# The order of SyncE's transfers in a graph transformer layer

## The chip, the cores and the metric

The kernel runs on one core of a Trainium2 chip. The metric is the time of one execution on the device in microseconds, and the median of the runs is quoted.

## What is computed

Four message-passing layers over one graph of 6,250 nodes with 256 features and 106,250 edges, sorted by destination: two graph convolutions, a graph attention layer with four heads, and a graph transformer layer. The change touches the last, and one transfer in the first:

```
q = x1 @ Wq + bq;  k = x1 @ Wk + bk;  v = x1 @ Wv + bv
logits2 = einsum('ec,ec->e', q[d2], k[s2]) / sqrt(256)
alpha2 = segment_softmax(logits2, d2)
out = segment_sum(v[s2] * alpha2[:, None], d2)
out = prelu(out + x1 @ Wskip + bskip)
```

## The kernel before

The edges are cut into 52 groups of 2,048, each as 16 steps (u = 0 to 15) of 128 edges. As edges are sorted by destination, the destinations of a group lie in a window of 128 nodes. `relrow`, in HBM, holds for each edge its place in that window as int16; it is written once in the first layer (lines 292 to 294) from the tile `rr` of seven columns of 128, of which the last is filled to 64 partitions only.

The last layer (`transformer_layer`, line 1772) works on three groups at a time, each at another stage. In pass k it scores group k, works out the softmax maxima of group k-1 (the "chain"), and sums group k-2 (the "agg"). `passes` (line 1809) writes out the first three passes and the last ones, and runs a loop over bodies of eight passes between. Every engine has a `body` for one pass; `parts` (line 1822) says which stages it has; `lead` is the preparation of group k+1.

- GpSimd gathers the source rows of each step from HBM into one of four buffers `G` (line 1841), as soon as the group four back is summed.
- TensorE does for each step a score matmul (L2198: the window `win` picked out by the one-hot `ohT` into `psA`) and an aggregation matmul (L2208), and between them the small transposes of the chain. It waits for the window of its group once, ahead of step 0 (line 2233). Score(u) waits until dot(u-2) is done.
- VectorE does for each step a dot product (L1943: `G` with `psA`), and the one-hot of the next group (L1918). It builds `ohT` (L1923) in four parts at steps 7, 10, 13 and 15 from `relb`, the row of places copied to all 128 partitions. At step 4 it scans with the mask `mkr` (L2031). At steps 1 to 12 it works out the node results of group k-2; the last of them is L1983, after which `s_res` is raised. A pass ends with two scans (L2142, L2146).
- ScalarE takes the exponentials and weighs the one-hots.
- SyncE issues the transfers. It handles them in program order and waits at semaphores in between. Per group there are the places (`relb`, 512 KB, four buffers, L1868), the window (`win`, 128.5 KB, two buffers, L1865), the mask (`mkr`, 1.5 KB, two buffers, L1885), the loads of `skip` and `xa` for the next node block (128 KB each, L1848 and L1849) and the store of the result (128 KB, L1855). Before the window of group k+1, SyncE waits until all scores of group k-1 are done (`s_pa`), before the places for a maximum of an earlier group (`s_s1`), before the mask for `s_s2`. The loads and the store wait for `s_res` (`turn`, line 1857).

So SyncE's body k, before, is: places of k+1, window of k+1, mask of k, extra windows if a group needs them, then `turn` for the group k-2: wait for `s_res`, loads, store.

Of the kernel before, what the change touches and what calls it, by code (L numbers as in the profile page):

```python
# [22 lines left out]
P = 128  # L23
# [8 lines left out]
NC = NG * U  # L32
# [8 lines left out]
UW = 16  # L41
GW = UW * P
NGW = NC // UW
# [58 lines left out]
def hold(m, eng):  # L102

    eng.sem_inc(m.held[str(eng.engine)], 1)  # L104
# [6 lines left out]
def load_wide(nc, m, eng, g, keys):  # L111

    lim = {"d0": (0, 0, N - 1), "nwin": (1, 1, NT), "base": (2, 0, NGW + NT), "last": (3, 0, N - 1), "xb": (4, 0, NT)}
    return [nc.s_assert_within(eng.value_load(m.ctw[0:1, bass.ds(g * TW + k, 1)]) & TABLE_BITS, lo, hi,
                               skip_runtime_bounds_check_because=TABLE_FITS)
            for k, lo, hi in (lim[n] for n in keys)]


def first_layer(nc, m, a):
# [13 lines left out]
    with ExitStack() as c:  # L133
# [36 lines left out]
        rr = sb("rr", [P, NCH, P], I16)  # L170
# [29 lines left out]
        @block.gpsimd  # L200
        def _(pool):
            nc.gpsimd.memset(m.ones[:], 1.0)
            nc.gpsimd.memset(m.eps[:], LN_EPS)
            nc.gpsimd.memset(m.ident[:], 0.0).then_inc(s_set, 1)
            pool.wait_ge(s_set, 1)
            nc.gpsimd.affine_select(out=m.ident[:], in_=m.ident[:], compare_op=ALU.not_equal, fill=1.0,
                                    base=0, pattern=[[-1, P]], channel_multiplier=1)
            nc.gpsimd.iota(m.iota[:], [[1, P]], base=0, channel_multiplier=0, allow_small_or_imprecise_dtypes=True)
            nc.gpsimd.iota(m.iotap[:], [[1, 1]], base=0, channel_multiplier=1, allow_small_or_imprecise_dtypes=True)
            nc.gpsimd.memset(stage[:], 0.0)  # L210
            nc.gpsimd.memset(al[:], 0.0)
            nc.gpsimd.memset(h[:, :, D:AW], 0.0)
            nc.gpsimd.memset(zrow[:], 0.0).then_inc(s_set, 1)
            nc.gpsimd.memset(acc, 0.0).then_inc(s_accz, 1)
            pool.wait_ge(s_si, 16)
            pool.wait_ge(s_z1, 16)
            pool.wait_ge(s_ast, 16)
            for j in range(NLB):
                pool.wait_ge(s_t1[j], 16)
            for g in range(NGW):  # L220
                b = g % NBW
                width = D if g < NBW else AW
                if g >= NBW:
                    pool.wait_ge(s_done, g - NBW + 1)
                if g == NBW:
                    pool.wait_ge(s_col, 16)
                for u in range(UW):
                    pool.indirect_dma_start(G[:, b, u, 0:width], None, m.t1,  # L228
                                            IOA(ap=m.srcI[:, g * UW + u:g * UW + u + 1], axis=0)).then_inc(s_g[b][u // QW], 16)
            pool.wait_ge(s_done, NGW - NBW + 1)  # L230
            pool.wait_ge(s_fin, 16)
            for u in range(EARLY2):
                pool.indirect_dma_start(m.gathered(D)[:, 0, u, :], None, m.t2, IOA(ap=m.srcI[:, u:u + 1], axis=0)).then_inc(m.ahead2[u // QW], 16)

        @block.sync
        def _(sp):
# [53 lines left out]
            sp.dma_start(part[:], m.wsum.rearrange("(g n) -> g n", n=SLOTS)).then_inc(s_part, 16)  # L290
            sp.wait_ge(s_rr, 1)
            places = m.relrow.rearrange("(c w e) -> w c e", w=P, e=P)
            sp.dma_start(places[:, 0:NC // P, :], rr[:, 0:NC // P, :]).then_inc(s_z, 16)
            sp.dma_start(places[0:NC % P, NC // P, :], rr[0:NC % P, NC // P, :]).then_inc(s_z, 16)
            sp.wait_ge(s_dis, 1)
            with nc.allow_non_contiguous_dma(reason="three columns of the table"):
                sp.dma_start(rows(m.t1)[:, :, D:AW], facs[:]).then_inc(s_col, 16)
# [27 lines left out]
            with sp.Fori(0, NGW) as k:  # L325
                d0, last = load_wide(nc, m, sp, k, ("d0", "last"))
                nwin, past = load_pack(nc, m, sp, k)
                base = past + k
# [4 lines left out]
            base, last = load_wide(nc, m, sp, NGW, ("base", "last"))  # L333
# [5 lines left out]
            sp.wait_ge(s_st, base * ST + (ST + 16))  # L339
            sp.wait_ge(s_fin, 16)  # L340
            hold(m, sp)
            sp.wait_ge(s_z, 16 * 9)

        @block.vector
        def _(dve):
# [1426 lines left out]
def transformer_layer(nc, m):  # L1772
# [4 lines left out]
    with ExitStack() as c:  # L1777
# [7 lines left out]
        mkr = sb("mkr", [1, 2, 3 * (P + 1)])  # L1785
# [11 lines left out]
        s_mk = [sem(f"mk{b}") for b in range(2)]  # L1797
# [24 lines left out]
        def parts(k):  # L1822
            if not isinstance(k, int):
                return True, True, True, True
            return k < NGW, 1 <= k <= NGW, k >= 2, k + 1 < NGW
# [3 lines left out]
        @block.gpsimd  # L1829
        def _(pool):  # L1830
            nc.gpsimd.memset(run[:], -BIG)
            nc.gpsimd.memset(Lb[:], -BIG)
            nc.gpsimd.memset(stage[:], 0.0).then_inc(s_zero, 1)
            for g in range(NGW):
                b = g % NBW
                if g >= NBW:
                    pool.wait_ge(s_ok, g - NBW + 1)
                for u in range(EARLY4 if g == 0 else 0, UW):
                    if g >= NBW and u % QW == 0:
                        pool.wait_ge(s_aq, (g - NBW) * NQ + u // QW + 1)  # L1840
                    pool.indirect_dma_start(G[:, b, u, :], None, m.t4, IOA(ap=m.srcI[:, g * UW + u:g * UW + u + 1],  # L1841
                                                                           axis=0)).then_inc(s_g[b][u // QW], 16)

        @block.sync
        def _(sp):

            def load(n, start):
                sp.dma_start(skip[:], m.sk[bass.ds(start, P), :]).then_inc(s_own, 16)  # L1848
                sp.dma_start(xa[:], m.xa[bass.ds(start, P), :]).then_inc(s_own, 16)  # L1849

            def store(n, start):
                sp.wait_ge(s_res, n + 1)
                sp.wait_ge(s_st, n * ST + ST)
                hold(m, sp)
                sp.dma_start(m.out[bass.ds(start, P), :], o[:]).then_inc(s_st, 16)  # L1855

            def turn(n, start, before):
                sp.wait_ge(s_res, n + 1)
                hold(m, sp)
                load(n + 1, start)  # L1860
                store(n, before)

            def window(k, r):
                d0, = load_wide(nc, m, sp, k, ("d0",))
                sp.dma_start(win[:, r, :], m.qk[bass.ds(d0, P), :]).then_inc(s_win[r], 16)  # L1865

            def places(k, b):
                sp.dma_start(relb[:, b % 4, :], m.relrow[bass.ds(k * (UW * P), UW * P)].partition_broadcast(P)).then_inc(s_rb[b % 4], 16)  # L1868

            def body(k, kq, kh, b, past):  # L1870
                logits, chain, agg, lead = parts(k)
                if lead:
                    if not (isinstance(k, int) and k < 3):
                        sp.wait_ge(s_s1, k - 2)
                        hold(m, sp)
                    places(k + 1, b + 1)
                    if agg or chain:
                        sp.wait_ge(s_pa, k * UW)
                        hold(m, sp)
                    window(k + 1, (b + 1) % 2)  # L1880
                if logits:
                    if agg:
                        sp.wait_ge(s_s2, k - 1)
                        hold(m, sp)
                    sp.dma_start(mkr[:, b % 2, :], m.rmask[bass.ds(k * (3 * (P + 1)), 3 * (P + 1))]  # L1885
                                 .rearrange("(a n) -> a n", a=1)).then_inc(s_mk[b % 2], 16)
                    d0, = load_wide(nc, m, sp, k, ("d0",))
                    nwin, xb = load_pack(nc, m, sp, k)
                    with sp.If(nwin > 1):
                        with sp.Fori(1, nwin) as i:  # L1890
                            sp.wait_ge(s_xpa, (xb + i - 1) * UW + 1)
                            hold(m, sp)
                            sp.dma_start(winx[:], m.qk[bass.ds(window_start(nc, d0, i), P), :]).then_inc(s_xwin, 16)
                if agg:
                    d0, last = load_wide(nc, m, sp, k - 2, ("d0", "last"))
                    nwin, xb = load_pack(nc, m, sp, k - 2)
                    base = xb + (k - 2)
                    turn(base, d0, last)
                    with sp.If(nwin > 1):
                        with sp.Fori(1, nwin) as i:  # L1900
                            turn(base + i, window_start(nc, d0, i), window_start(nc, d0, i - 1))

            sp.sem_inc(s_xpa, 1)
            sp.sem_inc(s_st, ST)
            places(0, 0)
            window(0, 0)
            load(0, 0)
            passes(sp, body)
            base, last = load_wide(nc, m, sp, NGW, ("base", "last"))
            store(base, last)  # L1910
            sp.wait_ge(s_st, (base + 2) * ST)
            hold(m, sp)
# [521 lines left out]
```

## Time and profile before

| | |
|---|---|
| median of 3 runs | 6158.78 us (6152.38 to 6185.52) |
| the profiled execution, its span | 6170.1 us, 6168.3 us |
| busy: TensorE, VectorE, GpSimd, ScalarE | 3904.2, 2719.5, 3232.2, 718.2 us |
| mean granted TensorE clock | 0.762 |
| SyncE's queue | 170437 packets, 185.56 MB |
| GpSimd's queue | 159744 packets, 441.43 MB |

The page of the profile shows these for one execution. The span is the time from its first to its last instruction. Beside the page, the trace was asked for busy time by stretch, for who waited for whom, and for timelines of single engines. In a timeline a row has the start, the length, engine, line and operation, what it writes and reads, and in brackets how long the engine was idle before it and what ended this. A wait for several semaphores is put down to the one that came last by the profile, which can be another than the real one. DVE is VectorE, PE is TensorE, POOL is GpSimd, SPq is SyncE's queue.

### The profile page before, as it was taken

To read this page: it belongs to the slowest core of one execution; us is meant where nothing else is said; L and a number is where in the kernel's file an instruction comes from. 1 tells how busy PE (TensorE), PEld (TensorE's weight loads), DVE (VectorE), ACT (ScalarE), POOL (GpSimd) and SP (SyncE) were. 2 spreads that over 40 slices of the span, in tenths; PEclk is the share of its full clock that TensorE was granted. 3 is DMA by queue.
4 is the path that set the end of the run, shared out by engine and by line. 5 is a ranking of instruction groups with operands and counts; after the bars stand their busy time and mean duration, and the time that the engine had idled before them with its cause. 6 is when DMAs were issued, how large, how long until landed. Compare 5 with 4: busy or idle time off the path is not lost. (4 is left out here: it accounts for less than half of the span.)

```text
span 6168.3 us, 73822 instructions
## 1 busy us (share of the span) xinstructions
PE 3904.2 (63%) x14562; PEld 2847.0 (46%) x14563; DVE 2719.5 (44%) x9904; ACT 718.2 (12%) x2361; POOL 3232.2 (52%) x3351
## 2 busy tenths in 40 slices
PE   3555555563556655554667666767674777777777
PEld 2343434342444444443455555555552555555555
DVE  5443434342333233332444444444453555555555
ACT  3000000000000000000111111101110212222122
POOL 5466666644555555554444444444433555555553
PEclk8677777776777777776777776777786888888889
DMA  7344444433333333332333333333322444343432
GB/s 182 80 107 106 107 105 107 106 86 88 106 107 106 106 107 107 107 101 87 89 94 97 93 97 93 96 95 95 96 78 84 113 119 122 111 119 112 118 115 84
DMA packets 334355, 636.43 MB, mean 103 GB/s; under 512 B 86166, under 2 KB 213124, under 8 KB 333828
## 3 DMA queue, kind: packets, MB, share of 16 engines
q0 software_dynamic: 159744, 441.43, 27.5%
q1 hardware_dynamic: 170437, 185.56, 9.6%
q8 instruction: 177, 2.90, 0.2%
q10 hardware_dynamic: 3648, 3.67, 0.2%
q14 instruction: 349, 2.86, 0.2%
HBM read 565.59 MB, written 64.79 MB: 102 GB/s over the span
## 5 line engine op out<-in xcount | busy, mean ns | idle before, releaser
L1211 POOL DMA_INDIRECT G<-t,srcI x828 | 807.6, 975 | 914.2 <-DVE g_Gp L1425 676.3
L1841 POOL DMA_INDIRECT G<-t,srcI x824 | 785.7, 953 | 629.6 <-PE g_ps L2208 371.7
L228 POOL DMA_INDIRECT G<-t,srcI x832 | 820.7, 986 | 516.1 <-issue 238.7
L859 POOL DMA_INDIRECT G<-t,srcI x828 | 793.6, 958 | 536.7 <-ACTq L1133 298.8
L2198 PE MATMUL g_psA<-g_win,g_ohT 128*128 128x257 f32 x1664 | 614.1, 456 | 374.7 <-DVE g_L L1943 177.6
L737 PE MATMUL g_ps<-G,g_oh 128*128 128x257 f32 x1664 | 555.6, 500 | 142.8 <-DVE g_oh L587 142.8
L1554 PE MATMUL g_psA<-g_win,g_ohT 128*128 128x4 f32 x1664 | 345.1, 328 | 439.1 <-issue 416.4
L1943 DVE CUSTOM_DVE_ANT_0 g_junk<-G,g_psA 128x257 f32<-128x257 f32 x832 | 348.5, 419 | 557.9 <-DMA G<-t,srcI 239.2
L1554 PEld LDWEIGHTS g_psA<-g_win,g_ohT 128*128 128x128 f32 x1664 | 359.6, 316 | 459.6 <-issue 459.1
L2208 PE MATMUL g_ps<-G,g_oh 128*128 128x257 f32 x1664 | 558.2, 422 | 0.0
L2198 PEld LDWEIGHTS g_psA<-g_win,g_ohT 128*128 128x128 f32 x1664 | 321.7, 217 | 511.2 <-DVE g_L L1943 222.6
L737 PEld LDWEIGHTS g_ps<-G,g_oh 128*128 128x128 f32 x1664 | 415.7, 258 | 290.2 <-DVE g_oh L587 186.4
L1088 PE MATMUL g_ps<-G,g_oh 128*128 128x256 f32 x1664 | 510.6, 455 | 0.0
L1601 PE MATMUL g_ps<-g_Gp,g_oh 128*128 128x264 f32 x1664 | 412.4, 396 | 21.3 <-issue 21.1
L1088 PEld LDWEIGHTS g_ps<-G,g_oh 128*128 128x128 f32 x1664 | 376.9, 235 | 96.2 <-issue 33.9
L2208 PEld LDWEIGHTS g_ps<-G,g_oh 128*128 128x128 f32 x1664 | 352.3, 215 | 84.8 <-issue 24.9
L1314 DVE TENSOR_TENSOR g_oh<-iota,g_relx 128x512 f32<-128x512 f32 x208 | 136.0, 689 | 560.1 <-DMA G<-t,srcI 500.7
L1601 PEld LDWEIGHTS g_ps<-g_Gp,g_oh 128*128 128x128 f32 x1664 | 313.6, 193 | 97.3 <-issue 44.0
L966 DVE TENSOR_SCALAR g_oh<-iota,g_relx,g_wx 128x128 f32<-128x128 f32 x832 | 228.7, 349 | 185.9 <-DMA G<-t,srcI 89.7
L594 DVE SCALAR_TENSOR_TENSOR g_a<-g_own,g_stage 128x256 f32<-128x256 f32 x53 | 25.7, 485 | 567.4 <-ACT g_stage L809 566.0
L587 DVE TENSOR_SCALAR g_oh<-iota,g_relx,g_wx 128x128 f32<-128x128 f32 x832 | 240.3, 362 | 32.5 <-issue 22.8
L2300 ACT ACTIVATE g_oh<-g_oh,g_p 128x128 f32<-128x128 f32 x832 | 248.7, 387 | 6.4
(372 smaller groups left out, 4825.9 us busy)
## 6 DMA issues: line engine op xcount, KB each, us to landing
G<-t,srcI POOLq DMA_INDIRECT x3328
g_relb<-relrow SPq DMA_DIRECT2D x104, 512.0 KB
t<-g_t SPq DMA_DIRECT2D x53, 132.0 KB, 1.7
g_rec<-t SPq DMA_DIRECT2D x53, 132.0 KB
g_own<-t SPq DMA_DIRECT2D x53, 129.5 KB
x<-g_o SPq DMA_DIRECT2D x53, 128.5 KB
g_rec<-x SPq DMA_DIRECT2D x53, 128.5 KB
t<-g_t4r SPq DMA_DIRECT2D x53, 128.5 KB, 2.0
```

The costliest lines, as they stand in the source:

```text
L228: pool.indirect_dma_start(G[:, b, u, 0:width], None, m.t1, IOA(ap=m.srcI[:, g * UW + u:g * UW + u + 1], axis=0)).then_inc(s_g[b][u // QW], 16)
L737: last = nc.tensor.matmul(ps[:, 0:CW], oh[:, u, :], G[:, b, u, 0:CW], start=(u == 0), stop=(u == UW - 1))
L859: pool.indirect_dma_start(G[:, b, u, :], None, table, IOA(ap=m.srcI[:, g * UW + u:g * UW + u + 1], axis=0)).then_inc(s_g[b][u // QW], 16)
L1088: last = nc.tensor.matmul(ps[:, 0:D], oh[:, u, :], G[:, b, u, :], start=(u == 0), stop=(u == UW - 1))
L1211: pool.indirect_dma_start(G[:, b, u, :], None, m.t3, IOA(ap=m.srcI[:, g * UW + u:g * UW + u + 1], axis=0)).then_inc(s_g[b], 16)
L1554: last = nc.tensor.matmul(psA[:, u * H:u * H + H], ohT[:, u, :], win[:, b % 2, :], start=True, stop=True)
L1601: last = nc.tensor.matmul(ps[:, 0:AGW], oh[:, b1, u, :], Gp[:, b1, u, :], start=(u == 0), stop=(u == UW - 1))
L1841: pool.indirect_dma_start(G[:, b, u, :], None, m.t4, IOA(ap=m.srcI[:, g * UW + u:g * UW + u + 1], axis=0)).then_inc(s_g[b][u // QW], 16)
L1943: nc.vector.tensor_tensor_reduce(out=junk[:, u % 2, :], in0=G[:, b, u, :], in1=psA[:, u % 2, 0:RW], scale=1.0, scalar=0.0, op0=ALU.mult, o ...
L2198: nc.tensor.matmul(psA[:, u % 2, 0:RW], ohT[:, u, :], win[:, r, :], start=True, stop=True).then_inc(s_pa, 1)
L2208: last = nc.tensor.matmul(ps[:, r, 0:RW], oh[:, b2, u, :], G[:, b2, u, :], start=(u == 0), stop=(u == UW - 1))
L2300: last = nc.scalar.activation(src[:, u, :], src[:, u, :], ACT.Copy, scale=p[:, r, u:u + 1])
```

## The change

In the last layer SyncE's body k waits for the result of group k-2 (`s_res`) first, and then issues the window of group k+1, the loads and the store of `turn`, the places of group k+2 (instead of k+1) and the mask of group k. Ahead of the loop two rows of places are issued, for groups 0 and 1. For the wait of the places, `s_s1` is asked for k-1 instead of k-2. In passes 0 and 1, which have no result to wait for, the rest is issued in the same order. Extra windows of the group stay ahead of all this; no group of this input needs one.

In the first layer GpSimd sets the last column of `rr` to zero, so that `relrow` is stored whole with one transfer instead of two.

```diff
             nc.gpsimd.memset(al[:], 0.0)
+            nc.gpsimd.memset(rr[:, NC // P, :], 0)
...
-            sp.dma_start(places[:, 0:NC // P, :], rr[:, 0:NC // P, :]).then_inc(s_z, 16)
-            sp.dma_start(places[0:NC % P, NC // P, :], rr[0:NC % P, NC // P, :]).then_inc(s_z, 16)
+            sp.dma_start(places, rr[:]).then_inc(s_z, 16)
...
-            sp.wait_ge(s_z, 16 * 9)
+            sp.wait_ge(s_z, 16 * 8)
...
             def body(k, kq, kh, b, past):
                 logits, chain, agg, lead = parts(k)
-                if lead:
-                    if not (isinstance(k, int) and k < 3):
-                        sp.wait_ge(s_s1, k - 2)
-                        hold(m, sp)
-                    places(k + 1, b + 1)
-                    if agg or chain:
-                        sp.wait_ge(s_pa, k * UW)
-                        hold(m, sp)
-                    window(k + 1, (b + 1) % 2)
                 if logits:
-                    if agg:
-                        sp.wait_ge(s_s2, k - 1)
-                        hold(m, sp)
-                    sp.dma_start(mkr[:, b % 2, :], m.rmask[bass.ds(k * (3 * (P + 1)), 3 * (P + 1))]
-                                 .rearrange("(a n) -> a n", a=1)).then_inc(s_mk[b % 2], 16)
                     d0, = load_wide(nc, m, sp, k, ("d0",))
...
                     base = xb + (k - 2)
-                    turn(base, d0, last)
+                    sp.wait_ge(s_res, base + 1)
+                    hold(m, sp)
+                if lead:
+                    if agg or chain:
+                        sp.wait_ge(s_pa, k * UW)
+                        hold(m, sp)
+                    window(k + 1, (b + 1) % 2)
+                if agg:
+                    load(base + 1, d0)
+                    store(base, last)
+                if lead:
+                    if not isinstance(k, int) or k + 2 < NGW:
+                        if not (isinstance(k, int) and k < 2):
+                            sp.wait_ge(s_s1, k - 1)
+                            hold(m, sp)
+                        places(k + 2, b + 2)
+                if logits:
+                    if agg:
+                        sp.wait_ge(s_s2, k - 1)
+                        hold(m, sp)
+                    sp.dma_start(mkr[:, b % 2, :], m.rmask[bass.ds(k * (3 * (P + 1)), 3 * (P + 1))]
+                                 .rearrange("(a n) -> a n", a=1)).then_inc(s_mk[b % 2], 16)
...
             places(0, 0)
+            places(1, 1)
             window(0, 0)
```

## Rows read from the trace of the kernel before

**Rows 1.** Busy time in a stretch of the last layer: window, length, engines, clock, DMA.
```profile
5050.00:5400.00 350.00, 262.98 (x997) 189.31 (x998) 202.91 (x948) 74.15 (x245) 194.78 (x205) 0.88 0.41 115
```

**Rows 2.** Tile view of the window: score matmuls, durations, first and last start.
```profile
L2198 PE MATMUL g_psA<-g_win,g_ohT x1664: 378/380/797, 4690.1 to 6137.4; 128*128 128x257 f32 x185
```

**Rows 3.** Waits from 4800 to 6100 us: total, times, longest.
```profile
POOL G L1841 <- PE g_ps L2208: 345.1, 114, 6.1
...
DVE g_junk L1943 <- PE g_psA L2198: 155.7, 151, 3.8
```

**Rows 4.** Timeline of VectorE, one pass: start, length, line, idle before.
```profile
5314.87 0.42 DVE L1983 TENSOR_TENSOR g_o<-g_o,g_v 128x256 f32<-128x256 f32 x1
...
5320.31 0.42 DVE L1943 CUSTOM_DVE_ANT_0 g_junk<-G,g_psA 128x257 f32<-128x257 f32 x1 [1.08 <-issue]
```

**Rows 5.** Timeline of SyncE's queue, the same pass.
```profile
5315.61 0.37 SPq L1848 DMA_DIRECT2D g_skip<-sk  x1
...
5318.49 0.36 SPq L1855 DMA_DIRECT2D out<-g_o  x1
5320.12 0.01 SPq L1868 DMA_DIRECT2D g_relb<-relrow  x1
5323.14 0.71 SPq L1865 DMA_DIRECT2D g_win<-qk  x1
5326.03 0.01 SPq L1885 DMA_DIRECT2D g_mkr<-rmask  x1
```

**Rows 6.** Timeline of TensorE, the same pass.
```profile
5318.06 0.69 PE L2198 MATMUL g_psA<-g_win,g_ohT 128*128 128x257 f32 x2
```

**Rows 7.** Timelines of VectorE and TensorE, the shortest and the longest distance.
```profile
4905.91 0.41 DVE L1983 TENSOR_TENSOR g_o<-g_o,g_v 128x256 f32<-128x256 f32 x1
...
4908.86 0.70 PE L2198 MATMUL g_psA<-g_win,g_ohT 128*128 128x257 f32 x2 [0.29 <-issue]
...
5010.73 0.42 DVE L1983 TENSOR_TENSOR g_o<-g_o,g_v 128x256 f32<-128x256 f32 x1
...
5018.64 1.22 PE L2198 MATMUL g_psA<-g_win,g_ohT 128*128 128x257 f32 x2 [4.42 <-issue]
```

**Rows 8.** Timeline of SyncE's queue, one pass later.
```profile
5346.96 0.34 SPq L1868 DMA_DIRECT2D g_relb<-relrow  x1
5348.12 0.64 SPq L1865 DMA_DIRECT2D g_win<-qk  x1
```

**Rows 9.** The page, part 6: issues of transfers, KB each, median us to landing.
```profile
t<-g_t SPq DMA_DIRECT2D x53, 132.0 KB, 1.7
...
t<-g_t4r SPq DMA_DIRECT2D x53, 128.5 KB, 2.0
```

**Rows 10.** Timelines of VectorE and SyncE, a tight pass.
```profile
5097.51 0.46 DVE L1983 TENSOR_TENSOR g_o<-g_o,g_v 128x256 f32<-128x256 f32 x1
...
5107.07 0.28 SPq L1885 DMA_DIRECT2D g_mkr<-rmask  x1
...
5108.28 0.47 DVE L2031 TENSOR_TENSOR_SCAN g_run<-g_mkr,g_run,g_psR 1x128 f32<-1x128 f32 x1
```

**Rows 11.** Timelines of SyncE's queue and VectorE, start of the layer.
```profile
4685.24 0.35 SPq L1868 DMA_DIRECT2D g_relb<-relrow  x1
4686.17 0.35 SPq L1865 DMA_DIRECT2D g_win<-qk  x1
...
4689.57 1.71 DVE L1923 TENSOR_SCALAR g_ohT<-g_relb,iotap 128x512 f32<-128x512 int16 x4 [3.42 <-DMA g_relb<-relrow]
```

**Rows 12.** Timeline of GpSimd, start of the kernel.
```profile
0.73 0.20 POOL L202 MEMSET ones<- 128x128 f32 x1 [0.29 <-POOLq L2428]
```

**Rows 13.** Timeline of VectorE: three dots with a wait, idle before in brackets.
```profile
4808.79 0.42 DVE L1943 CUSTOM_DVE_ANT_0 g_junk<-G,g_psA 128x257 f32<-128x257 f32 x1 [2.46 <-PE g_psA L2198]
...
5310.00 0.42 DVE L1943 CUSTOM_DVE_ANT_0 g_junk<-G,g_psA 128x257 f32<-128x257 f32 x1 [3.66 <-DMA G<-t,srcI]
...
5992.90 0.42 DVE L1943 CUSTOM_DVE_ANT_0 g_junk<-G,g_psA 128x257 f32<-128x257 f32 x1 [2.70 <-PE g_psA L2198]
```

More of the change, by code:

```diff
@@ L1897, in body @@
                     base = xb + (k - 2)
-                    turn(base, d0, last)
+                    sp.wait_ge(s_res, base + 1)
[20 more added lines that the diff above has]
+                                 .rearrange("(a n) -> a n", a=1)).then_inc(s_mk[b % 2], 16)
+                if agg:
                     with sp.If(nwin > 1):
```

## The prediction

> **What bounds the kernel now.** I started with the granted clock and busy time by stretch. In a steady 350 us of the last layer, TensorE is busy 75% at a granted clock of 0.88, VectorE 58% and GpSimd 56% [rows 1]. So none of them is full. The score matmuls of that layer run from 4690.1 to 6137.2 us [rows 2], which over 52 groups is 27.8 us per group, and only this layer changes much. Next come the waits. VectorE's dots wait for TensorE 151 times and GpSimd for TensorE's aggregation 114 times [rows 3]. TensorE and VectorE form a ring: a dot needs its score, and score(u) may run only two dots ahead. No row has anyone of size waiting for a SyncE transfer. The transfers are off the path now, and the question is whether the change puts one on it.
>
> So I put SyncE's queue beside the ring. One group's batch begins when VectorE's last node step (L1983) ends: at 5314.87 + 0.42 = 5315.29 [rows 4]. SyncE issues skip at 5315.61, the store at 5318.49, the relative row (places) at 5320.12, the window at 5323.14 and the mask at 5326.03 [rows 5]. **The kernel before already issues all of these in one burst behind the result**, because the next body's lead-in follows the previous turn at once. What the program calls two groups ahead is therefore, in time, the burst in which the row leaves today: before, body k+1 sends the row of k+2, after, body k does, both behind the result of pass k. The same goes for load and store. Two things really move: the window and the mask each leave one whole group later (window k+1 behind the result of pass k, not k-1), and inside the burst the window goes from last but one to first.
>
> **Window, the main term.** When is it needed? Score(0) of the next pass starts at 5318.06 in this pass, 2.77 us after the result [rows 6]. Over the 47 passes that begin between 4.8 and 6.1 ms this distance runs from 2.54 us (4905.91 + 0.41 to 4908.86) to 7.49 us (5010.73 + 0.42 to 5018.64) [rows 7]; I put them in order and the middle one is 3.4. VectorE can absorb some lateness, since it scans and reads its table there: score(0) ends at 5318.06 + 0.69 = 18.75 but dot(0) starts at 5320.31 [rows 4, 6]. For dot(1), the smaller margin of the two, I found 1.0 to 1.6 us in the tight passes. I take 1.2.
>
> When does it land? SyncE needs about four small steps from result to skip issue, 0.32 us (5315.29 to 5315.61) [rows 4, 5]. The window needs those and a table read. From the row's issue to the window's is 1.16 us where SyncE is quick (5346.96 to 5348.12) and 3.02 us where it is slow (5320.12 to 5323.14) [rows 5, 8]. Without the row's own issue (0.34, 0.7) that is 0.8 to 2.3 us, so with the 0.32 the window leaves 1.1 to 2.7 us after the result. Nearest transfers of 128 KB: 1.7 and 2.0 us from issue to landing [rows 9]. Landing is then 2.8 to 4.7 us after the result; I also allow 6, for gathers that share the engines. I then ran every one of the 47 passes through max(0, landing - start of score(0) - its margin). The sums: landing at 3.5 us costs 0; at 4.0, 1 us in all; at 4.5, 5 us; at 5.0, 14; at 5.5, 25; at 6.0, 39. **I take 4.5, so +5 us**, nearest to the slow SyncE rows since 5315 and most passes look like them; ends 0 and +39.
>
> Here the Trainium skill speaks against the change: DMA: Bandwidth & Descriptors, Rules for kernel authors, says to issue a DMA early, compute, and wait late. The trace agrees that the present order has no window wait. The same page (Anatomy of one DMA, a fit for GpSimd's path) gives 2.0 us plus bytes over 436e3; for 131,584 B that is an estimate of 2.3 us against the 1.7 and 2.0 of the rows. By it landings would be 0.3 to 0.6 later and the term about +10 instead of +5.
>
> **Mask.** It too loses a group of lead, and it is now behind the 512 KB row instead of the window. Its reader is the forward scan at step 4 (L2031). In a tight pass the result ends at 5097.51 + 0.46 = 5097.97, the mask is issued at 5107.07 and the scan runs at 5108.28 [rows 10]; today that scan reads the mask of the burst before, afterwards it would read this one, 1.2 us after its issue. The issue keeps its place in the burst, but the row ahead of it leaves some 1.5 us later than now: 5320.12 - 5315.29 = 4.8 [rows 4, 5] becomes 6.3, and with the 4.3 us that the first row of the layer took (below) it is in at 10.6 us after the result, against a scan at 10.3 here. No row shows the mask's own landing. Bounds: 0, where step 4 is later (the scan comes after 11 us in most passes), and 1.0 us in each of the 12 tightest, +12. Behind a mask wait stand VectorE's next dots. I take +3, near the low end, as a pass made late by the window has its scan late too.
>
> **Row, load, store.** The row slips behind window, loads and store by about 1.5 us; its reader, the first ohT build of a pass, comes at step 7, three steps after that scan, and the one row wait that I found is at the layer's start (3.42 us [rows 11]). Load and store move by the same 1.5 us; readers are steps 6 and 11. Cost 0; if that cover were gone, one transfer per group, 2 us or about 100 in all.
>
> **Layer start.** Rows 0 and 1 now go ahead of window 0. Row issue at 4685.24, window at 4686.17 [rows 11], first score at 4690.1 [rows 2]. One more issue (0.93 us) and one more 512 KB: the row took 4.3 us to the first ohT build (4689.57 [rows 11]), less the 2.0 of a small one, 2.3 us. The first score is held by ohT anyway. Between 0 and +3.3; I take +1.
>
> **First layer.** One transfer issue fewer on SyncE, whose issues take 0.3 to 0.7 us each [rows 5, 8], and one memset of 128 x 128 more on GpSimd (0.20 us for one of float32 [rows 12]). Both are one-off steps in the opening of a 6 ms kernel: between -0.7 and +0.2, taken as 0.
>
> **Sum.** 5 + 3 + 1 + 0 = +9 us. Against the profiled execution, 6170.1 us with a span of 6168.3, that is 6179; this execution is 11.3 us (0.2%) above the median of 6158.8, and the terms do not scale with that, so the forecast for the median is 6158.8 + 9 = **6168 us**, +0.15%. A measurement of this kernel can tell about 0.5% (31 us) from no change, so the likely verdict is "same".
>
> **Rivals.** (1) *Nothing measurable moves at all.* The window lands by 3.5 us and the mask before the scan: 6160. For it: the quick SyncE rows, and that the burst is already one. (2) *The window wait becomes the new turn of the ring, slower.* It decides from a landing of about 5.7 us after the result, where the sum passes 31. For it: in slow stretches SyncE takes 3.02 us for steps that it does elsewhere in 1.16, the window now leaves behind such steps, and gathers share its engines. Against: in 28 of the 47 passes score(0) starts later than 3.0 us after the result. Price 39 at 6 us plus 4 for mask and start: 6202; the skill's early-issue rule above would point here. (3) *A gain.* VectorE waits about 2.5 us for TensorE at step 3 or 4 in 13 passes (2.46 the first, 2.70 the last [rows 13]), just when the tail of the burst, window and mask, is in flight. If that is the transfers' doing and goes with the window's move: 13 x 2.4 = 31 less, +9, gives 6137. Against: longer waits stand at steps 8 and 9, where SyncE issues nothing (3.66 us at 5310.00 [rows 13]; that row names a gather, but step 9 waits for no gather), and the big transfer stays.
>
> **How the numbers follow.** Forecast as worked out 0.50 and rival 1 0.20, both inside 0.5%; rival 2 0.18; rival 3 0.07; 0.05 for what I have not seen, slower by 0.02 and faster by 0.03. So faster 0.10, same 0.70, slower 0.20. The range goes from rival 3 to rival 2: 6138 to 6204.
>
> **What would show it.** Right: the window first in SyncE's burst, 1.1 to 2.7 us after L1983 ends; new, short TensorE idle times ahead of score(0) put down to the window's transfer, in under half of the passes, and L2031 with a wait under 1 us in some; distance from result to dot(0) in tight passes (5.0 now) at most 6; the spacing of row and load unchanged. Wrong: dot(0) at 6.5 or more in most passes (rival 2); no window wait at all (rival 1); or step 3 and 4 waits gone (rival 3). The prediction fails as a whole if the long waits at steps 8 and 9 hang on SyncE's transfers after all, for then every shift in the burst counts, in either direction.

## The result, and the profile after

The changed kernel took 6184.51 us in the median (6161.43 to 6210.51), the kernel before, run beside it, 6168.45. The ratio is 1.003, with an interval of 1.0022 to 1.0039: **18.5 us slower**, 0.3%, inside the 0.5% that I had called "same". (Differences in us are here and below the ratio applied to the time of before.) I had forecast +9. The size of the effect is twice the forecast, and this section and the next find where the other half sits.

One execution scatters by more than the effect. The profiled one of the changed kernel took 6174.2 us with a span of 6172.4, only 4 us above that of before, so sums over one trace say how the work moved, and the medians say what it cost.

The window's tile view of the changed kernel answers [rows 2] (form, durations in ns, first and last start). L2207 is the score matmul; the changed file is nine lines longer there. The lines under it say what its engine had waited for, in us and times:
```profile
L2207 PE MATMUL g_psA<-g_win,g_ohT x1664: 377/380/797, 4688.0 to 6141.3; 128*128 128x257 f32 x185
...
  DMA g_win<-qk: 55.1, 19
```
The layer's score matmuls run over 1453.3 us instead of 1447.3. And there is a wait that the kernel before had nowhere inside the layer: TensorE waits for the window's transfer.

Waits of the changed kernel from 4800 to 6100 us, the same view as [rows 3] (total, times, longest):
```profile
POOL G L1841 <- PE g_ps L2217: 368.5, 127, 6.2
...
DVE g_junk L1952 <- PE g_psA L2207: 140.9, 159, 4.5
...
PE g_psA L2207 <- DMA g_win<-qk: 31.0, 17, 3.1
...
DVE g_run L2040 <- DMA g_mkr<-rmask: 0.3, 1, 0.3
```
The profile puts 17 passes, 31.0 us in all, down to the window. That count is a low one: of many window transfers this trace holds only some of the 16 events that tell of completion, and the wait is then called "issue". Without names, TensorE stands idle for over 1 us ahead of score(0) in 35 of 46 passes, where before it did so in 6 of 48 (five of these six are the turns of the loop, every eighth pass, and they stay). The mask is waited for once, for 0.3 us. The row of places, the loads and the store stand in no wait of the steady part.

A steady stretch, as in [rows 1], barely differs; clock 0.87 instead of 0.88:
```profile
5050.00:5400.00 350.00, 262.09 (x986) 191.81 (x985) 201.52 (x934) 73.90 (x244) 193.67 (x203) 0.87 0.41 114
```

Now one pass. SyncE's queue after the result of a tight pass, which answers [rows 5]. The result (L1992, L1983 before) ends at 5096.11 + 0.42 = 5096.53:
```profile
5098.88 0.69 SPq L1865 DMA_DIRECT2D g_win<-qk  x1
5099.67 0.44 SPq L1848 DMA_DIRECT2D g_skip<-sk  x1
5100.20 0.38 SPq L1849 DMA_DIRECT2D g_xa<-xa  x1
5102.00 0.01 SPq L1855 DMA_DIRECT2D out<-g_o  x1
5102.77 0.71 SPq L1868 DMA_DIRECT2D g_relb<-relrow  x1
```
The order is the new one, window first, and the window leaves 2.35 us after the result. TensorE and VectorE of the same pass, as in [rows 4, 6]:
```profile
5096.78 0.60 PE L2207 MATMUL g_psA<-g_win,g_ohT 128*128 128x257 f32 x2
...
5101.36 0.70 PE L2207 MATMUL g_psA<-g_win,g_ohT 128*128 128x257 f32 x2 [1.96 <-issue]
...
5102.45 1.06 PE L2207 MATMUL g_psA<-g_win,g_ohT 128*128 128x257 f32 x2
```
```profile
5100.28 0.19 DVE L2155 TENSOR_TENSOR_SCAN g_W<-mk,g_F 128x16 f32<-128x16 f32 x1 [0.24 <-DVE g_F L2151]
5102.09 0.42 DVE L1952 CUSTOM_DVE_ANT_0 g_junk<-G,g_psA 128x257 f32<-128x257 f32 x1 [1.62 <-PE g_psA L2207]
...
5103.56 0.42 DVE L1952 CUSTOM_DVE_ANT_0 g_junk<-G,g_psA 128x257 f32<-128x257 f32 x1 [0.83 <-PE g_psA L2207]
```
Score(0) starts 4.83 us after the result, where a tight pass of before had 2.54 to 2.77 [rows 6, 7], and VectorE, done with its scans at 5100.47, waits 1.62 us for it. The profile puts TensorE's 1.96 us down to "issue" here, so this pass is none of the 17; the trace holds 4 of the 16 completion events of its window. As score(0) starts 2.48 us after the window's issue, and in the 17 passes the same distance is 2.38 in the middle (1.1 to 4.1), I read it as a wait for the window all the same.

A second price shows in the same rows: score(1) takes 1.06 us where the matmuls ahead of the wait took 0.60, and dot(1) waits another 0.83. Over 49 passes, score(1) takes over 1.0 us in 20; before it did so in 7. Busy time and clock by stretch (PE is the first busy time, the clock the third number from the end):
```profile
5098.50:5101.30 2.80, 0.90 (x4) 0.30 (x2) 1.20 (x6) 0.39 (x1) 1.21 (x3) 1.00 0.59 165
5101.30:5105.00 3.70, 3.64 (x10) 2.95 (x11) 1.32 (x7) 0.00 (x0) 2.72 (x3) 0.62 0.83 234
```
After a stretch in which TensorE was busy for 0.90 of 2.80 us, the granted clock falls from 1.00 to 0.62 in the mean of the next 3.7 us, so mostly its 1.2 GHz level, and the first steps of the pass go at that pace.

Over all passes that have a result ahead of them (49 or 50), the middle distances from the result, before and after: window issue 7.48 and 2.77 us (before, that one was meant for the pass after next, a whole group earlier); score(0) 3.5 and 5.38; dot(0) 6.34 and 6.91; places issue 4.94 and 6.22; mask issue 9.25 and 7.12; mask scan 11.78 and 11.95. The median period of a pass goes from 27.26 to 27.55.

The layer's start answers [rows 11]: two rows of places, then the window, and the wait for the places is as long as before.
```profile
4681.43 0.83 SPq L1868 DMA_DIRECT2D g_relb<-relrow  x2
4682.84 0.34 SPq L1865 DMA_DIRECT2D g_win<-qk  x1
...
4685.73 1.67 DVE L1932 TENSOR_SCALAR g_ohT<-g_relb,iotap 128x512 f32<-128x512 int16 x4 [3.38 <-DMA g_relb<-relrow]
```
From the first row to the first score is 4688.0 - 4681.43 = 6.6 us; before it was 4690.1 - 4685.24 = 4.9 [rows 2, 11]. So the second row costs up to 1.7 us, once, which no median here can resolve.

### The profile page after: what moved, and what is told of

Read it like the earlier page. It is cut to its first block and busy times, and to the rows that moved or that the text cites. A ratio compares the mean times of both kernels' runs of the same rounds, so it can differ in the third digit from the quotient of the medians.

```text
span 6172.4 us, 73818 instructions
## 1 busy us (share of the span) xinstructions
PE 3919.8 (64%) x14562; PEld 2866.9 (46%) x14563; DVE 2718.8 (44%) x9904; ACT 718.8 (12%) x2361; POOL 3231.6 (52%) x3352
## 3 DMA queue, kind: packets, MB, share of 16 engines
q0 software_dynamic: 159744, 441.43, 27.4%
q10 hardware_dynamic: 3648, 3.67, 0.2%
## 5 line engine op out<-in xcount | busy, mean ns | idle before, releaser
L2207 PE MATMUL g_psA<-g_win,g_ohT 128*128 128x257 f32 x1664 | 626.0, 464 | 390.6 <-DVE g_L L1952 167.7
L737 PE MATMUL g_ps<-G,g_oh 128*128 128x257 f32 x1664 | 556.4, 500 | 141.9 <-DVE g_oh L587 141.9
L2207 PEld LDWEIGHTS g_psA<-g_win,g_ohT 128*128 128x128 f32 x1664 | 333.5, 222 | 513.3 <-issue 231.1
L2217 PE MATMUL g_ps<-G,g_oh 128*128 128x257 f32 x1664 | 569.8, 430 | 0.0
```

The source lines that it names most:

```text
L737: last = nc.tensor.matmul(ps[:, 0:CW], oh[:, u, :], G[:, b, u, 0:CW], start=(u == 0), stop=(u == UW - 1))
L2207: nc.tensor.matmul(psA[:, u % 2, 0:RW], ohT[:, u, :], win[:, r, :], start=True, stop=True).then_inc(s_pa, 1)
L2217: last = nc.tensor.matmul(ps[:, r, 0:RW], oh[:, b2, u, :], G[:, b2, u, :], start=(u == 0), stop=(u == UW - 1))
```

## The experiments

**Parts of the change.** Four kernels ran beside the kernel before, at 6143.52 us there. `e1_window_late` makes one part alone: the kernel before, but with the window behind the result.

```diff
-                    if agg or chain:
-                        sp.wait_ge(s_pa, k * UW)
-                        hold(m, sp)
-                    window(k + 1, (b + 1) % 2)
+                    if not agg:
+                        if chain:
+                            sp.wait_ge(s_pa, k * UW)
+                            hold(m, sp)
+                        window(k + 1, (b + 1) % 2)
...
-                    turn(base, d0, last)
+                    sp.wait_ge(s_res, base + 1)
+                    hold(m, sp)
+                    if lead:
+                        sp.wait_ge(s_pa, k * UW)
+                        hold(m, sp)
+                        window(k + 1, (b + 1) % 2)
+                    load(base + 1, d0)
+                    store(base, last)
```


> The kernel before with one thing changed: the window of group k+1 is issued behind the result, first in the burst, as in the changed kernel; places, mask and the first layer stay as they were. Theory (the window wait is the cost): ratio to before 1.002 to 1.004 (+12 to +25 us), TensorE waits for the window in 15 or more passes. Rival (the cost is the mask behind the row, or the order of the burst as a whole): 1.000 to 1.001.

Measured: 6166.73 us, ratio 1.0039 (1.0026 to 1.0051), +24 us. Waits of the layer's steady part (4800 to 6100 us), in an execution of 6137.98 us, the fastest of the six: the row shows where TensorE waits, and only the medians show the price.
```profile
PE g_psA L2206 <- DMA g_win<-qk: 40.6, 22, 3.6
```
The window alone costs what the whole change costs.

`e2_window_early` is the converse: the changed kernel with everything in its new place but the window, which leaves ahead of the wait for the result again.

```diff
+                if lead:
+                    if agg or chain:
+                        sp.wait_ge(s_pa, k * UW)
+                        hold(m, sp)
+                    window(k + 1, (b + 1) % 2)
                 if logits:
                     d0, = load_wide(nc, m, sp, k, ("d0",))
...
                     sp.wait_ge(s_res, base + 1)
                     hold(m, sp)
-                if lead:
-                    if agg or chain:
-                        sp.wait_ge(s_pa, k * UW)
-                        hold(m, sp)
-                    window(k + 1, (b + 1) % 2)
```


> The changed kernel with the window issued again ahead of the result, one group earlier; everything else as changed. Theory (the window wait is the cost): ratio to before 0.9995 to 1.001, no wait for the window. Rival (mask behind the row, places, first layer): stays at 1.002 to 1.004.

Measured: 6143.08 us, ratio 0.9996 (0.9987 to 1.0005), and no wait for the window in the steady part. Undoing this part undoes the loss, to within an interval of -8 to +3 us.

`e3_row_whole` makes the edit of the first layer alone, in the kernel before (the memset and the two hunks of the diff about `rr` and `s_z`).

> The kernel before with the first layer's part of the change alone: last column of rr set to zero, relrow stored with one transfer. Every theory: ratio 1.000, within 0.001. A ratio above 1.002 would mean that the cost lies there and not in the last layer.

Measured: 6147.66 us, ratio 1.0005 (0.9994 to 1.0016): nothing.

`e4_mask_early` is the changed kernel with the mask issued early again, ahead of the wait for the result.

```diff
                 if logits:
+                    if agg:
+                        sp.wait_ge(s_s2, k - 1)
+                        hold(m, sp)
+                    sp.dma_start(mkr[:, b % 2, :], m.rmask[bass.ds(k * (3 * (P + 1)), 3 * (P + 1))]
+                                 .rearrange("(a n) -> a n", a=1)).then_inc(s_mk[b % 2], 16)
+                if logits:
                     d0, = load_wide(nc, m, sp, k, ("d0",))
...
-                if logits:
-                    if agg:
-                        sp.wait_ge(s_s2, k - 1)
-                        hold(m, sp)
-                    sp.dma_start(mkr[:, b % 2, :], m.rmask[bass.ds(k * (3 * (P + 1)), 3 * (P + 1))]
-                                 .rearrange("(a n) -> a n", a=1)).then_inc(s_mk[b % 2], 16)
```


> The changed kernel with the mask issued again one group earlier, ahead of the wait for the result; window late. Theory (the window wait is the cost, the mask term that I put at +3 us is near 0): ratio 1.002 to 1.004, as the change itself. Rival (the mask behind the 512 KB row costs a third or more): 1.001 to 1.002.

Measured: 6167.81 us, ratio 1.0041 (1.0028 to 1.0054). With the mask out of the way nothing is won back. The interval is 16 us wide, too wide to tell my +3 from 0; the one mask wait of 0.3 us in the changed kernel's trace is what says that it was nearly 0.

**The size of the lag.** `e5_window_last` takes the window from the front of the burst to its end, behind the 512 KB row; nothing else changes:

```diff
-                if lead:
-                    if agg or chain:
-                        sp.wait_ge(s_pa, k * UW)
-                        hold(m, sp)
-                    window(k + 1, (b + 1) % 2)
                 if agg:
                     load(base + 1, d0)
...
                                  .rearrange("(a n) -> a n", a=1)).then_inc(s_mk[b % 2], 16)
+                if lead:
+                    if agg or chain:
+                        sp.wait_ge(s_pa, k * UW)
+                        hold(m, sp)
+                    window(k + 1, (b + 1) % 2)
```

`e6_table_ahead` takes the other direction: SyncE reads the window's address from its table before it waits for the result, so that the window leaves sooner.

```diff
                     base = xb + (k - 2)
+                    if lead:
+                        dw, = load_wide(nc, m, sp, k + 1, ("d0",))
                     sp.wait_ge(s_res, base + 1)
                     hold(m, sp)
...
-                    window(k + 1, (b + 1) % 2)
+                    if agg:
+                        sp.dma_start(win[:, (b + 1) % 2, :], m.qk[bass.ds(dw, P), :]).then_inc(s_win[(b + 1) % 2], 16)
+                    else:
+                        window(k + 1, (b + 1) % 2)
```


> The changed kernel with the window issued last in the burst, behind row and mask. In the changed kernel the mask's issue is at 7.1 us after the result in the median; a window issued there lands at about 10. By the step model of the prediction (landing less start of score(0) less 1.2 us, summed over 47 passes; score(0) started at 3.9 us in the mean) that is 5 us a pass: +200 to +260 us, ratio 1.032 to 1.042. Rival (the ring absorbs most of it, since its long waits at steps 8 and 9 move into the wait): under +120 us, ratio under 1.02.

> The changed kernel with the read of the window's table entry moved ahead of the wait for the result, so that between result and window issue two slow steps fewer stand (0.7 to 1.0 us). Theory (the window wait is the cost, and each microsecond of landing counts by the step model): landing at about 4.6 instead of 5.4, which is worth 12 to 15 us: ratio 1.0005 to 1.0015, fewer than 15 passes with a wait for the window. Rival (the table read is hidden): 1.003 as the change.

These two ran where **the kernel before takes 4492.73 us**, 27% less than in the runs above. I call it the quick level, and the other the common one; the expectations call them chips. It does not go with the number of the chip: the runs name chip 2 for 6143.52 and for 4492.73 us, and chip 4 for 4495.68 and for 6094.64. What decides the level, no run tells. There the late window (last) took 4843.58 us, ratio 1.0783 (1.0762 to 1.0804), +352 us; the table ahead 4513.34, ratio 1.005 (1.0033 to 1.0066). Both miss what was expected of them, +200 to +260 us and 1.0005 to 1.0015; these figures were worked out from the common level's passes. The first of them in the waits (3430 to 4700 us) and in one pass of SyncE and TensorE:
```profile
PE g_psA L2207 <- DMA g_win<-qk: 330.8, 45, 8.8
```
```profile
4125.65 1.90 SPq L1868 DMA_DIRECT2D g_relb<-relrow  x1
...
4129.08 0.36 SPq L1865 DMA_DIRECT2D g_win<-qk  x1
```
```profile
4134.36 1.22 PE L2207 MATMUL g_psA<-g_win,g_ohT 128*128 128x257 f32 x2 [8.64 <-DMA g_win<-qk]
4136.23 1.07 PE L2207 MATMUL g_psA<-g_win,g_ohT 128*128 128x257 f32 x2
4137.77 0.60 PE L2207 MATMUL g_psA<-g_win,g_ohT 128*128 128x257 f32 x2
```
Behind the row it takes 5.3 us from issue to use in this pass (5.0 in the middle of all), and TensorE stands still for up to 8.8 us. The first two scores then go at the lower clock (1.22 and 1.07 us against 0.60). This is rival 2 at full size: the window as the turn of the ring.

To have the change itself at this level, I ran it there again, with the table ahead and with the window early beside it (`e7_change_again` is the changed kernel, `e8_table_ahead_2` the edit of `e6_table_ahead`, `e9_window_early_2` that of `e2_window_early`).

> The changed kernel as it is, beside the next two on one chip. On a chip on which the kernel before takes about 6150 us: ratio 1.002 to 1.004. On a chip on which it takes about 4490 us, where SyncE's steps between result and window issue take 0.45 us less table read instead of 2.8: by the window theory window landing at about 3.3 us after the result, passes are shorter too, ratio 1.004 to 1.008, at least that of the kernel with the table read ahead (1.005 there).

> The changed kernel with the table read ahead of the wait for the result, beside the change on the same chip. Window theory: 0.001 to 0.002 below the change on a chip at about 6150 us, where a table read costs SyncE some 0.7 to 1 us; 0.001 to 0.003 below it on a chip at about 4490 us, where it costs 0.4 us in every pass (0.4 x 48 = 19 us at most, 0.004). Rival (table read hidden): the same as the change.

> The changed kernel with the window issued one group earlier again, on the same chip as the change. Window theory: ratio to before 0.9990 to 1.0010 on either chip, no idle time of TensorE that the window ends. Rival (on a quick chip the burst itself or the mask costs too): above 1.002.

Measured, with before at 4495.68: the change 4529.42, ratio 1.0081 (1.0061 to 1.01), +36 us, at the upper end of the 1.004 to 1.008 expected; the table ahead 4515.3, ratio 1.0052 (1.0032 to 1.0071), +23; the window early 4498.37, ratio 1.0012 (1.0 to 1.0025). The waits for the window from 3430 to 4400 us, of the change and of the table ahead:
```profile
PE g_psA L2207 <- DMA g_win<-qk: 81.5, 40, 3.3
```
```profile
PE g_psA L2212 <- DMA g_win<-qk: 41.9, 29, 3.0
```
Window early has no such wait there. So the cause is the same at both levels and the price differs. SyncE is quicker here, the window leaves 0.86 us after the result instead of 2.77, but the whole ring is quicker too: score(0) could start at 2.75 us (window early), and starts at 4.55 in the change, 3.29 with the table ahead. The 4.55 lies between two groups, as the passes alternate: about 3.6 us in one and 5.0 in the next, the window taking about 2.7 and about 4.0 us from issue to use; why it alternates, no run shows. The table read moves the window by 0.40 us. All six runs with the table ahead (up to 4523.21 us) are below all five of the change (from 4526.89), so that it helps is shown; by how much (about 13 us) is not settled, as the two ratios' intervals overlap. The trace shows half the window's waiting time and a distance to score(0) shorter by 1.3 us in the middle and 0.7 in the mean, but the profiled execution is the fastest of the six (4490.99 us) and may flatter it.

`e12_window_last_2` repeats the window at the end of the burst at the common level (before 6094.64 us).

> The changed kernel with the window issued last in the burst, once more, for the chip on which it was not tried. On a chip at about 4490 us: 1.078 again. On a chip at about 6150 us: mask issue stands at 7.1 us there, landing at about 10; the step model gives 200 to 260 us. Less than on the quick chip (351 us) in either case if a later pass head takes over part of the waits at steps 3 to 5 and 9, as between before and the change (126 to 62 us ahead of steps 3 to 5): under +200 us, ratio under 1.032.

Measured: 6298.08 us, ratio 1.0333 (1.0311 to 1.0356), +203 us. The same move that costs 352 us at the quick level costs 203 here, although score(0) starts at about the same distance after the result (9.13 us, 9.57 there). A part of that is a larger lag: score(0) comes 5.3 us later than before in the mean of 49 passes here, and 6.4 later than with the window early there. The time alone does not settle the rest: 203 lies at the foot of the 200 to 260 that the step model gave without any waits given back, and just above the 200 under which they would have shown. VectorE's waits, summed by step over 46 passes from the trace, show waits given back: at step 0 they rise from 88 us to 234, at steps 3 to 5 they fall from 126 to 33, and at step 9 they stay at 150 and 165. At this level there are waits at steps 3 to 5 into which a late start disappears; at the quick one they are 31 us in all, with the window early.

**Where those later waits come from.** They were the point on which I had said that the prediction would fail as a whole, so two kernels of before thin the gathers. `e10_thin_gathers` leaves the number of gathers and cuts their bytes; `e11_one_in_four` leaves out three gathers of four in the last layer.

```diff
-                    pool.indirect_dma_start(G[:, b, u, :], None, m.t4, IOA(ap=m.srcI[:, g * UW + u:g * UW + u + 1],
+                    pool.indirect_dma_start(G[:, b, u, 0:64], None, m.t4, IOA(ap=m.srcI[:, g * UW + u:g * UW + u + 1],
```


> The kernel before with the last layer's gathers cut to 64 of 257 columns: a quarter of the bytes, the same number of gathers and of rows. What it leaves out: most of the data that the dots and sums read. On a chip at about 6150 us, where VectorE waits about 150 us in all ahead of step 9: if those waits come from the gathers' bytes, they fall by more than half and the time by 60 us or more; if they come from GpSimd's issuing or the rows' number, they stay. On a chip at about 4490 us: no change (GpSimd issues back to back there, 1.25 us each), within 20 us.

```diff
+                    if u % QW:
+                        continue
...
-                            dve.wait_ge(s_g[b][q], kq * GL + GL)
+                            dve.wait_ge(s_g[b][q], kq * 16 + (GL if b == 0 and q * QW < EARLY4 else 16))
```


> The kernel before with one gather in four issued in the last layer; what it leaves out: three quarters of the gathered rows. On a chip at about 6150 us: if GpSimd's gathers cause the long waits ahead of steps 3, 4, 8 and 9 and SyncE's slow steps (0.7 us each), both go, 27 us a group become about 20, -300 us or more; if they have another cause, the layer stays above 25 us a group. On a chip at about 4490 us: the layer is no longer held to 20 us a group by GpSimd; the ring then sets it, 17 to 20 us, 0 to -150 us.

Measured, with before at 6094.64: a quarter of the bytes 6092.54, ratio 0.9993 (0.9972 to 1.0014), nothing; a quarter of the gathers (two runs) 5701.13, ratio 0.9353 (0.9327 to 0.9379), -394 us. Steady stretches of the two, with the columns of [rows 1]:
```profile
5050.00:5400.00 350.00, 270.47 (x995) 193.85 (x996) 203.00 (x952) 75.01 (x247) 193.45 (x204) 0.85 0.25 60
```
```profile
5100.00:5450.00 350.00, 316.93 (x1368) 233.10 (x1368) 273.34 (x1299) 103.30 (x340) 67.98 (x71) 0.98 0.28 83
```
With bytes cut, 60 GB/s instead of 115, the pace stays (x995 matmuls, x997 before). With gathers left out, TensorE does x1368 in the same 350 us and the clock is 0.98. That is the pace of the quick level, where all gathers are made (window early):
```profile
3700.00:4050.00 350.00, 316.00 (x1372) 232.02 (x1372) 277.38 (x1302) 103.51 (x341) 265.29 (x279) 0.99 0.57 159
```
VectorE's waits at step 9 fall from 150 us to 20 with the gathers left out (154 with bytes cut, 19 at the quick level), the mean period from 27.4 us to 19.9 (20.3 there). So the long later waits hang on the number of gathers, neither on their bytes nor on SyncE's burst, whose transfers are all there in `e11_one_in_four`. Whether it is GpSimd's issuing or the number of rows fetched, these two runs don't part, as both fall together; and why the quick level makes all of them without this price, no run tells.

## Why the prediction was right, and where its size was off

**The burst.** Right: one burst behind the result before and after, window from last but one to first, and only window and mask a group later. `e2_window_early` shows the rest of the burst to cost 3 us at most; at the quick level, 1.0 to 1.0025 leaves up to 11 us open.

**The window's issue.** Forecast 1.1 to 2.7 us after the result. Measured 2.77 in the middle of all passes, 2.89 in the 17 that wait for it: just past the slow end of my range. The slow SyncE rows were the right ones to take, but I misread them: I took 0.7 us off for the row's own issue, which lasts 0.01 us there [rows 5], so that these rows put the window at 0.32 + 3.01 = 3.3 us after the result. Up to 3.67 were measured.

**The window's landing: the term that was mis-sized.** I took 1.7 and 2.0 us to landing from [rows 9], let score(0) start at the landing, and put that at 4.5, which is about 2.7 + 1.8. From issue to a score(0) that waits for it is 2.38 us in the middle of those 17 passes (1.1 to 4.1), and the score starts at 5.45. In seven of the 17 the trace holds all 16 completion events of the transfer. The last of them comes 1.4 to 2.4 us after the issue, 2.0 in the middle, as the row said, and score(0) starts 0.37 to 0.47 us behind it. So the sum is 2.9 + 2.0 + 0.4 = 5.3: the largest single piece that was missing is the 0.4 us from landing to score, which I had put at nothing. The landing also scatters; part 6 of the changed kernel's page reads, for the kind of transfer that had 2.0 before:
```profile
t<-g_t4r SPq DMA_DIRECT2D x53, 128.5 KB, 2.4
```
My own model of 47 passes gives 14 us for a landing at 5.0 and 25 at 5.5, so about 23 for 5.4, where I had put 5; measured were +18.5 (change) and +24 (`e1_window_late`). Its sums come out with each pass's own margin; with 1.2 us for all, as the prediction can be read, they would be 10 us at 4.5 and 38 at 5.5. The steepness was on the page that I wrote: 5 us at 4.5, 25 at 5.5. A range of half a microsecond in the input ought to have put the middle of the forecast at 14 and not at 5.
The Trainium skill, DMA: Bandwidth & Descriptors, Anatomy of one DMA, gives the estimate of 2.3 us that I had set beside the rows. The seven landings are at 2.0 in the middle and not at 2.3; the 2.38 us hold the start of the score as well. That the +10 that I worked out from it lay nearer than my +5 is chance.

**What the model lacks.** Two things of opposite sign, so that it comes near at the common level is in part luck. The clock falls in many passes with the idle time ahead of score(0), and dot(1) and dot(2) of a late pass follow by 1.4 and 1.1 us in the middle, up to 1.7, instead of 0.55 and 0.68. And steps 3 to 5 give back: VectorE waits there for 62 us in all instead of 126, while steps 0 to 2 rise from 108 to 150 and step 9 from 150 to 176; all steps together 487 instead of 481. Matched pass by pass, with the starts of score(0) of both traces, the model gives 24 us, and dot(3) comes 35 us later, summed over 49 passes.

At the quick level little gives back. There the model, matched in the same way with window early, gives 17 us for the change, but dot(3) comes 44 us later in sum, against +36 measured. The difference arises in steps 0 to 2, where score(1) takes over 1.0 us in 21 passes instead of 5. With the window last it is largest: in the mean of 49 passes dot(0) comes 5.0 us later than in window early and dot(3) 7.1, and the mean period grows by 7.1 (27.45 less 20.34).

**Mask.** Forecast +3. Wrong in a harmless direction: one wait of 0.3 us, `e4_mask_early` no faster. With the window ahead of it instead of the table read and window issue behind the row, its issue even comes sooner after the result than before (7.12 against 9.25 us), and its scan is no earlier.

**Row, load, store, first layer, start.** Forecast 0, 0, 0, 0 and +1. No wait appears for any of them; `e3_row_whole` shows the first layer at nothing, and the start's 1.7 us at most lie within my 0 to 3.3.

**The rivals.** Rival 1 (nothing moves) is excluded by 1.0022 at the low end, and by `e1_window_late` against `e2_window_early`. Rival 2 had the mechanism, and I had put its threshold at a landing of 5.7 us; the change stays just short of it (5.4). `e7_change_again`, at the quick level, crosses the 0.5% with a window that leaves earlier: the ring turns faster there, and from issue to use are 3.16 us instead of 2.38. My "in under half of the passes" was right by the names that the profile gives (17 of 46), but not by TensorE's idle time (35 of 46), and it would have been wrong there (40 of 45). My signs for it were mixed: dot(0) at 6.5 or more in most passes did come true (6.91), but it was 6.34 before, so the sign could tell little. Rival 3 saw something real, waits at steps 3 to 5 that go when the window moves. But it had the sign of cause wrong: they are no doing of the transfers (113 us of them stay with the window early and all the rest moved, 33 with the window last), they are slack that a late start eats.

The Trainium skill, DMA: Bandwidth & Descriptors, Rules for kernel authors, says to issue early and wait late. The runs agree: the window alone, issued one group later, costs 1.0039, and going back costs nothing. None of the versions that do all the work beats the kernel before; the best, window early, equals it.

## What to carry to other kernels

A prefetch that is moved behind a join has no lead left but the distance from that join to its first use, so take that distance from the trace pass by pass, put issue and landing against it, and read the forecast off the curve over the whole range of the landing, not off its middle. Add the time from landing to use, and to each late pass what the granted clock costs after the idle time; then look for later waits that give it back; where there were hardly any, the same move cost 1.7 times as much, a part of it because it also made a larger lag. When several transfers are moved together, ask of each what lead it had in time and not in groups: here four of the five kept theirs or had it to spare, and only one did all the damage.

## What the runs showed of the hardware that I had not expected

**Two levels of the same kernel.** Its median was 6168.45, 6143.52 and 6094.64 us in some sets of runs and 4492.73 and 4495.68 in others, with all runs of a set at one level. At the slower level, SyncE's small steps are of two speeds. The window's register move in the tile view (min/median/max ns), first the kernel before, then window early at the quick level:
```profile
L1865 SPq MOVE g_win<-qk x52: 2/29/717, 4686.1 to 6100.6; - x52
```
```profile
L1865 SPq MOVE g_win<-qk x52: 29/29/29, 3407.6 to 4421.9; - x52
```
A move of 29 ns in the middle takes up to 717, and 29 always at the other. A gather's issue takes 0.95 us at both, and one follows the other after 0.30 us. That the number of gathers decides the pace at the slower level (-394 us with a quarter of them) and their bytes do not (0.9993) is shown; what the gathers share with SyncE and TensorE is not.

**The clock within a pass.** A stretch of 2.8 us in which TensorE was busy for 0.90 is followed by a granted clock of 0.62 over 3.7 us, and score(1) takes 1.06 us instead of 0.60. So a wait of 2 us can cost more than its length; it does not always, as after the wait of 2.00 us ahead of the score at 4963.76 us score(1) takes 0.60.
